# A Mamba2 block with a small MLP: the MLP taken out of the mixer's loop into a phase of its own, the next block's front moved in between the scan's groups

## The chip, the cores and the metric

One Trainium2 chip, one of its cores, float32 in and out. The metric is the device time in microseconds (us) of one launch.

## What is computed

The reference, cut to what matters. `x` is (8, 1024, 256); the `c` modulation gives six rows of 256 for each of the 8 sequences (shift, scale and gate for each of the two halves).

```
xn  = LN(LN(x)*(1+scale_a)+shift_a)                 # LN: mean and variance over the 256
zxbcdt = xn @ in_proj_w                             # 256 -> 1312: z, x, B, C, dt
dt  = softplus(dt + dt_bias); xBC = silu(causal_conv1d(xBC, 4 taps))
y   = ssd_scan(x_ssm, dt, B, C, A)                  # 32 heads of 16, state 128
y   = (y + D*x_ssm) * silu(z);  y = y * rsqrt(mean(y^2)+eps) * rms_w
out = y @ out_proj_w + residual
h   = LN(out); h = relu(h @ mlp_w1 + b1) @ mlp_w2 + b2      # 256 -> 1024 -> 256, the small MLP
x1  = x + gate_a * (h + out)
# feed-forward: ternary weights, 256 -> 2x1024 (silu*gate) -> 1024 gelu -> 1024 gelu -> 256
```

## The kernel before, in words

The work is cut into 16 blocks of 512 tokens (`HALF`): 8 sequences `b`, two halves `u`. A block's 512 tokens lie as four chunks of 128 (`NC`). The program has three stages, each with its own set of engine programs that start together: `mamba` (its short set-up, then its loop), a check of the feed-forward's weights, and the loop of `feed_forward`. Every engine runs its own instructions in order; what passes between engines is counted on semaphores (`Handover`, `Count`). A wait therefore also holds back all that is behind it on the same engine.

**One round of the mixer's loop** (one block), as TensorE sees it:

- ten tiles of the input projection (lines 580 on, six 512-column products each: high and low halves of both operands, `product` at 540). ScalarE empties each tile (743, 745; silu for the z tiles, 750), VectorE runs 15 of the 18 steps of the convolution (981) and GpSimd the other three (833, 836).
- the transposes of dt, the decay and `ec` products (594 on), then the **scan**: four chunks `c` of eight groups `i` (four heads each). For a group TensorE makes the decay matrix (`decay`, 615), ScalarE a relu and an exp of it (779, 785), VectorE the product with `gm` (1089), and TensorE, three groups behind (`LAG`), the contribution `intra` (626). At group 1 of a chunk VectorE reads the last chunk's `yin` (`addends`, 1032, 1041): `yin` exists once, so `intra` of the new chunk waits for that. At groups 3, 4, 6, 7 follow the mean of squares, the residual (1063), the next chunk's operands and the new state.
- the output projection of the last two chunks, with the last residual (1063).
- **the tail, which is the small MLP**: VectorE normalises `o1` (894 to 903), TensorE transposes it (685), eight tiles of `m1` (48 products of 512 columns), ScalarE relu (796), GpSimd rounds to the high half (874), VectorE takes the low half (1121), then `m2` (96 products of 256 columns). Into this tail VectorE also puts the **front of the next block** in five parts: LN of `x` (part 0), scale (1), shift (2), the second LN (3), then `low`, and part 4, the softplus series with the cumulative sum (lines 931 to 950, 20 steps that each wait for the one before). Part 4 ends in `c_cum`, for which ScalarE waits ahead of everything in its next round (736), GpSimd as well (`cleft` copies, 823) and SP too (the `cright` transfers).
- VectorE adds, multiplies by the gate and adds `x` (1133, 1137, 1139), and SP stores `x1_d` (529).

PSUM: four banks `bank` in a ring for everything but the scan's `eb` (two) and `yin`, `yoff`. The front's transposes and dt use the `eb` banks in the tail.

**The weight check** (lines 1194 to 1248) loads the five feed-forward matrices, then ScalarE writes a rounded copy of pieces of 2048 columns (1228), VectorE counts where it differs (1237), TensorE sums. Its result chooses the type of the feed-forward's products. Nothing else runs beside it.

**The feed-forward** (1252 to 1492) is not touched, but for where its weights live and where its semaphores are started.

## Time and profile before

| what | us |
|---|---|
| median of the runs (3) | 3752.67 |
| lowest and highest | 3750.81, 3753.17 |
| span of the profiled execution | 3750.4 |
| TensorE busy in the span | 3007.2 (80%) |
| VectorE busy | 2087.3 (56%) |
| ScalarE, GpSimd busy | 1405.1 (37%), 1073.2 (29%) |

The profiled execution has no device time of its own in the records, so its span stands for it; the median is 2.3 us above the span. The page of the profile cuts the span into 40 equal slices; up to the 24th TensorE is busy for 6 to 8 tenths, from the 26th for 9 or more:

```
PE   1777777687687687686687784699999999999999
DVE  0576 ... (5 to 7 tenths, then 3 to 5)
```

(The second line is shortened in words.) Busy shares are means over a slice; which engine is late in it is seen only in a timeline or in what ended each wait.

### The profile page before, as it was taken

To read this page: it belongs to the slowest core of one execution; us is meant where nothing else is said; L and a number is where in the kernel's file an instruction comes from. 1 tells how busy PE (TensorE), PEld (TensorE's weight loads), DVE (VectorE), ACT (ScalarE), POOL (GpSimd) and SP (SyncE) were. 2 spreads that over 40 slices of the span, in tenths; PEclk is the share of its full clock that TensorE was granted. 3 is DMA by queue.
4 is the path that set the end of the run, shared out by engine and by line. 5 is a ranking of instruction groups with operands and counts; after the bars stand their busy time and mean duration, and the time that the engine had idled before them with its cause. 6 is when DMAs were issued, how large, how long until landed. Compare 5 with 4: busy or idle time off the path is not lost. (4 is left out here: it accounts for less than half of the span.)

```text
span 3750.4 us, 50178 instructions
## 1 busy us (share of the span) xinstructions
PE 3007.2 (80%) x16750; PEld 2270.0 (61%) x16750; DVE 2087.3 (56%) x3938; ACT 1405.1 (37%) x2342; POOL 1073.2 (29%) x1276
## 2 busy tenths in 40 slices
PE   1777777687687687686687784699999999999999
PEld 0455455455355455455455453587887878787877
DVE  5676676677677667667677675433333333333333
ACT  0543553553553553553453452322222222222222
POOL 4333234234234234233233232122222222222222
PEclk6888888888887888888888887799999999999999
DMA  2000000000000001001001002100000000000000
GB/s 92 2 16 6 26 16 15 17 16 24 8 16 30 2 16 30 1 16 30 1 16 30 1 16 96 48 12 13 11 18 18 11 13 11 13 11 13 11 13 17
DMA packets 69811, 72.27 MB, mean 19 GB/s; under 512 B 25816, under 2 KB 64472, under 8 KB 68960
## 3 DMA queue, kind: packets, MB, share of 16 engines
q1 hardware_dynamic: 64480, 69.45, 5.8%
q8 instruction: 110, 1.80, 0.2%
q10 hardware_dynamic: 5120, 0.19, 0.1%
q14 instruction: 101, 0.83, 0.1%
HBM read 51.22 MB, written 28.36 MB: 21 GB/s over the span
## 5 line engine op out<-in xcount | busy, mean ns | idle before, releaser
L1309 PE MATMUL fbank<-hid,fw 128*128 128x512 f32 x4096 | 966.0, 397 | 0.0
L1309 PEld LDWEIGHTS fbank<-hid,fw 128*128 128x128 f32 x4096 | 770.2, 188 | 186.7
L1459 DVE TENSOR_TENSOR hid<-fhf,hid 128x512 fp32r<-128x512 f32 x384 | 264.6, 689 | 708.4 <-POOL hid L1416 708.4
L1416 POOL TENSOR_SCALAR hid<-fhf 128x512 fp32r<-128x512 f32 x384 | 270.3, 704 | 1045.7 <-ACT fhf L1388 765.2
L626 PE MATMUL yin<-mh,xpad 128*32 128x128 f32 x4096 | 353.0, 295 | 188.5 <-DVE mh L1089 110.3
L1388 ACT ACTIVATE fhf<-fbank,sh 128x512 f32<-128x512 f32 x256 | 176.4, 689 | 706.4 <-PE fbank L1309 706.2
L626 PEld LDWEIGHTS yin<-mh,xpad 128*32 128x32 f32 x4096 | 201.9, 115 | 375.9 <-issue 207.6
L1089 DVE TENSOR_TENSOR mh<-hf,gm 128x512 f32<-128x512 f32 x256 | 181.7, 710 | 171.7 <-ACT hf L785 171.7
L850 POOL TENSOR_TENSOR yg<-yin_s,yoff_s 128x512 f32<-128x512 f32 x56 | 84.2, 1503 | 674.5 <-DVE yoff_s L1041 674.5
L1089 DVE TENSOR_TENSOR mh<-cacc,gm 128x512 f32<-128x512 f32 x256 | 175.3, 699 | 145.4 <-ACT cacc L785 137.2
L540 PE MATMUL bank<-ah,wm 128*128 128x512 f32 x512 | 189.0, 449 | 65.2 <-DVE al L956 65.2
L779 ACT ACTIVATE cacc<-eb 128x512 f32<-128x512 f32 x256 | 150.5, 594 | 239.1 <-PE eb L615 239.0
L540 PE MATMUL bank<-wm,hh 128*128 128x256 f32 x1024 | 215.1, 310 | 30.7 <-DVE hl L1121 29.1
L540 PE MATMUL bank<-ah,win 128*128 128x512 f32 x640 | 212.4, 410 | 15.0 <-issue 12.5
L615 PE MATMUL eb<-cright,cleft 99*128 99x512 bf16 x512 | 216.9, 434 | 6.7 <-ACT cacc L779 5.5
L1332 PE MATMUL fbank<-fah,fw 128*128 128x512 f32 x512 | 205.6, 402 | 12.3 <-DVE fhf L1467 8.8
L1332 PE MATMUL fbank<-fal,fw 128*128 128x512 f32 x512 | 203.9, 398 | 0.0
L540 PEld LDWEIGHTS bank<-wm,hh 128*128 128x128 f32 x1024 | 170.5, 206 | 53.4 <-DVE hl L1121 48.4
L540 PE MATMUL bank<-wout,yh 128*128 128x256 f32 x512 | 129.4, 351 | 72.7 <-DVE yl L1046 72.7
L1379 ACT ACTIVATE sa<-fbank,s 128x512 f32<-128x512 f32 x128 | 88.1, 690 | 261.5 <-PE fbank L1332 225.3
L981 DVE SCALAR_TENSOR_TENSOR mh<-cin,cw,mh 128x512 f32<-128x512 f32 x192 | 181.3, 944 | 8.2
L779 ACT ACTIVATE hf<-eb 128x512 f32<-128x512 f32 x256 | 152.3, 595 | 82.5 <-PE eb L615 82.5
(191 smaller groups left out, 5357.5 us busy)
## 6 DMA issues: line engine op xcount, KB each, us to landing
xs<-in_x SPq DMA_DIRECT2D x17, 512.0 KB, 3.5
fx<-x_d SPq DMA_DIRECT2D x17, 512.0 KB, 3.9
h_d<-in_h SPq DMA_DIRECT2D x16, 512.0 KB, 4.9
x_d<-xs SPq DMA_DIRECT2D x16, 512.0 KB, 3.0
fw<-h_d SPq DMA_DIRECT2D x2, 4096.0 KB, 20.7
out_x<-fx SPq DMA_DIRECT2D x16, 512.0 KB, 3.1
w_d<-in_w SPq DMA_DIRECT2D x24, 128.0 KB, 3.9
cright<-parts SPq DMA_DIRECT2D x192, 8.0 KB, 1.9
```

What stands on the lines that cost most here:

```text
L540: mm = pe.matmul(o, left[a], right[c], start=(first and n == 0), stop=(last and n == 2))
L615: mm = pe.matmul(eb[h_eb.slot(key)][:], cleft[:, c, :], cright[c % 2][:, G4 * i:G4 * (i + 1), :].rearrange("k h t -> k (h t)"), start=True ...
L626: mm = pe.matmul(yin[row:row + 2 * HD, h // HQ, :], xpad[c % 2][:, h // 2, h % 2, :, :].rearrange("s w d -> s (w d)"), mh[i % RING][:, j, ...
L779: nc.scalar.activation(es[i % RING].rearrange("s h t -> s (h t)"), eb[h_eb.slot(key)][:], ACT.Relu, scale=-1.0).then_inc(h_eb.free(key), 1)
L981: ins = dve.scalar_tensor_tensor(out=cacc[m][:], in0=cin[:, m, t:t + HALF], scalar=cw[:, m, t:t + 1], in1=cacc[m][:], op0=ALU.mult, op1=AL ...
L1089: dve.tensor_tensor(mh[i % RING][:], es[i % RING], gm[c % 2][:].unsqueeze(1).to_broadcast([P, G4, P]), ALU.mult).then_inc(h_mh.full(key), 1)
L1309: mm = pe.matmul(bank[banks.slot(key)][:], w[:, k, m * P:(m + 1) * P].bitcast(dt), h[:, k, :].bitcast(dt), start=(k + n == 0), stop=(k == ...
L1332: mm = pe.matmul(bank[banks.slot(key)][:], w[:, k, m * P:(m + 1) * P].bitcast(dt), h[:, k, :].bitcast(dt), start=(k + n == 0), stop=(k == ...
L1379: nc.scalar.activation(sa[m % 2][:], bank[banks.slot(key)][:], ACT.Silu, scale=s1[:, m:m + 1])\
L1388: nc.scalar.activation(hf[j % 3][:], bank[banks.slot(key)][:], ACT.Gelu, scale=s[:, m:m + 1]).then_inc(banks.free(key), 1)
L1416: pool.tensor_scalar(hid[i % 2][0][:, m, :], hf[j % 3][:], 1.0, 0.0, ALU.mult, ALU.add)\
L1459: dve.tensor_tensor(hid[i % 2][1][:, m, :], hf[j % 3][:], hid[i % 2][0][:, m, :].bitcast(F32), ALU.subtract).then_inc(c_lo.sem, 1)
```

## The change

It does six things.

1. The MLP leaves the loop. The mixer now ends a block by storing `o1` to DRAM (`o1_d`); `xs` and the gate are no longer needed in the loop, `res` and `parts` get two buffers. `hh`, `hl` and the tail's instructions are gone.
2. The front of the next block sits between groups of the scan: VectorE's parts 0 to 3 behind groups (1,3), (1,6), (2,2), (2,6), `low` behind (3,6); TensorE's two sets of transposes and the dt product behind `intra` of (2,7), (3,1) and (3,3), into a bank `front_bank` of their own; ScalarE's affines at (3,3) and (3,4), its softplus start at (3,7). Part 4 stands after the last residual.
3. The ring of PSUM banks is three instead of four.
4. A new phase `mlp` between mixer and feed-forward runs the 16 blocks unrolled, with two buffers each for `o1` (`ob`) and `x` (`xb`), three tiles for `m1`, one bank for the transposes, four sums for `m2`.
5. ScalarE makes high half and full value itself, by two reads of PSUM; GpSimd instead makes the residual base `(o1 + b2)*gate + x` in three operations of 1024 columns.
6. The weight check is spread over blocks 3 to 13 of the phase, 44 pieces of 512 columns, four a block, at tiles 2 to 5. The stage of its own is gone.

The mixer's part of the diff, cut:

```diff
+FRONT_AT = {"nT0": (2, 7), "affine0": (3, 3), "nT1": (3, 1), "affine1": (3, 4), "low": (3, 6),
+            "dt": (3, 3), "softplus": (3, 7)}
+FRONT_DVE = {(1, 3): 0, (1, 6): 1, (2, 2): 2, (2, 6): 3}
...
-    banks = Handover(sem, "bank", list(mamba_bank_order()), 4)
...
+    banks = Handover(sem, "bank", list(mamba_bank_order()), 3)
+    fronts = Handover(sem, "frontbank", [(u, part) for u in us for part in FRONT_TILES], 1)
...
+                            if (c, i) == FRONT_AT["nT0"]:
+                                front(*after_block(b, u), 0)
+                            if (c, i) == FRONT_AT["nT1"]:
+                                front(*after_block(b, u), 1)
+                            if (c, i) == FRONT_AT["dt"]:
+                                front_dt(*after_block(b, u))
...
+                        if (c, i) == FRONT_AT["affine0"]:
+                            affine(*after_block(b, u), 0)
+                        if (c, i) == FRONT_AT["affine1"]:
+                            affine(*after_block(b, u), 1)
+                        if (c, i) == FRONT_AT["softplus"]:
+                            front_dt(*after_block(b, u))
...
+                        if c in (0, 1):
+                            power(*after_block(b, u), c + 1)
...
+                        if c == NC - 2:
+                            high(*after_block(b, u))
...
+                            if (c, i) in FRONT_DVE:
+                                front(*after_block(b, u), FRONT_DVE[c, i])
+                            if (c, i) == FRONT_AT["low"]:
+                                low(*after_block(b, u))
...
-                    normalise(nrm, o1, b, u, 3 + NC, lambda ins: after(mark(ins))).then_inc(c_norm.sem, 1)
...
+                    front(*after_block(b, u), 4)
```

The phase `mlp`, cut to its loads and to what each engine does in block `n`:

```diff
+MLP_HF = 3
+PIECE = 512
+EARLY = KF - 2
+PIECES = [(i, o) for i, (k, n) in enumerate(FFN_SHAPES) for o in range(0, k * n, PIECE)]
+PIECES_FROM = 3
+PIECES_PER = 4
...
+def pieces_of(n, m):
+
+    p = (n - PIECES_FROM) * PIECES_PER + m - 2
+    return [p] if 2 <= m < 2 + PIECES_PER and 0 <= p < len(PIECES) else []
...
+            def load(n):
+                b, s = n // NU, n % 2
+                if n >= 2:
+                    sp.wait_ge(h_x.free(n), h_x.used_before(0, n))
+                sp.dma_start(ob[s][:], o1_d[b, rows_of(n), :].rearrange("(c p) d -> p c d", p=P))\
+                    .then_inc(h_o.full(n), 16)
+                sp.dma_start(xb[s][:], g["x"][b, rows_of(n), :].rearrange("(c p) d -> p c d", p=P))\
+                    .then_inc(h_x.full(n), 16)
+                if n % NU == 0:
+                    sp.dma_start(gate[b % 2][:], mod_d[b, 2 * D:3 * D].partition_broadcast(P))\
+                        .then_inc(h_gate.full(b), 16)
...
+            load(0)
+            load(1)
...
+            for n in blocks:
+                if n < len(ws):
+                    sp.dma_start(ws[n][:].rearrange("p k n -> p (k n)").bitcast(F32), g["ffn_d"][n])\
+                        .then_inc(s_w[n], 16)
+                sp.wait_ge(c_x1.sem, c_x1.at(0, n + 1))
+                sp.dma_start(x1_d[n // NU, rows_of(n), :].rearrange("(c p) d -> p c d", p=P), xb[n % 2][:])\
+                    .then_inc(h_x.free(n), 16)
+                if n + 2 < MLP_BLOCKS:
+                    load(n + 2)
...
+        @block.tensor
...
+            for n in blocks:
+                for m in range(KF):
+                    key = (n, m)
...
+                if n + 1 < MLP_BLOCKS:
+                    transposes(n + 1, 0)
+                for ks in (range(EARLY), range(EARLY, KF)):
+                    for c in range(NC):
...
+                        if ks[0] == 0 and c == 1 and n + 1 < MLP_BLOCKS:
+                            transposes(n + 1, 1)
...
+        @block.scalar
...
+                    nc.scalar.activation(hh[:, m, :], tile[tiles.slot(key)][:], ACT.Relu, bias=b1c[:, m:m + 1])\
+                        .then_inc(c_hh.sem, 1)
+                    if j >= MLP_HF:
+                        act.wait_ge(c_hl.sem, c_hl.at(0, j - MLP_HF + 1))
+                    nc.scalar.activation(hf[j % MLP_HF][:], tile[tiles.slot(key)][:], ACT.Relu, bias=b1c[:, m:m + 1])\
+                        .then_inc(tiles.free(key), 1)
+                    for p in pieces_of(n, m):
+                        i, o = PIECES[p]
+                        act.wait_ge(s_w[i], 16)
+                        if p:
+                            act.wait_ge(s_count, p)
...
+        @block.gpsimd
...
+                if n + 1 < MLP_BLOCKS:
+                    power(n + 1)
...
+                pool.tensor_tensor(ob[s][:], ob[s][:], b2r[:].unsqueeze(1).to_broadcast([P, NC, D]), ALU.add)\
...
+                pool.tensor_tensor(ob[s][:], ob[s][:], g_, ALU.mult).then_inc(c_base.sem, 1)
...
+                pool.tensor_tensor(ob[s][:], ob[s][:], xb[s][:], ALU.add).then_inc(c_base.sem, 1)
...
+        @block.vector
...
+                    dve.tensor_tensor(hl[:, m, :], hf[j % MLP_HF][:], hh[:, m, :].bitcast(F32), ALU.subtract)\
...
+                    for p in pieces_of(n, m):
+                        dve.wait_ge(s_round, p + 1)
+                        if p:
+                            dve.wait_ge(s_count, p)
+                        dve.scalar_tensor_tensor(out=differs[:], in0=weight(*PIECES[p]), scalar=0.0,
+                                                 in1=rounded[:].bitcast(F32), op0=ALU.add,
+                                                 op1=ALU.not_equal, accum_out=count[:, p:p + 1]).then_inc(s_count, 1)
+                    if n + 1 < MLP_BLOCKS:
                         if m == 1:
...
+                            variances(n + 1)
+                        if m == 5:
+                            normalise(n + 1)
...
+                for c in range(NC):
...
+                    dve.tensor_tensor(xb[s][:, c, :], acc[c][:, 0:D], gate[b % 2][:], ALU.mult)\
...
+                dve.tensor_tensor(xb[s][:], xb[s][:], ob[s][:], ALU.add).then_inc(c_x1.sem, 1)
```

`variances(n + 1)` begins with a wait for the load of `ob` of block n + 1; `transposes` waits for `normalise`.

## Rows read from the trace of the kernel before

**Rows 1.** Windows by stage: stretch, length, busy by engine, PE clock, DMA, GB/s.
```profile
86.60:2322.50 2235.90, 1649.14 (x10436) 1163.48 (x10432) 1551.30 (x3045) 1051.14 (x1875) 730.02 (x833) 0.84 0.05 15
2322.50:2379.30 56.80, 2.17 (x11) 1.67 (x11) 30.30 (x39) 23.62 (x14) 2.07 (x2) 0.50 0.62 228
2379.30:3750.40 1371.10, 1344.91 (x6272) 1101.33 (x6272) 463.22 (x792) 325.77 (x447) 302.69 (x416) 1.00 0.04 13
```

**Rows 2.** Lines 1063 and 1139: ns min/median/max, first and last start.
```profile
L1063 DVE SCALAR_TENSOR_TENSOR o<-bank,rms,res x64: 470/480/485, 156.2 to 2275.3; 128x256 f32<-128x256 f32 x64
L1139 DVE TENSOR_TENSOR xs<-xs,o x16: 1224/1224/1227, 230.2 to 2318.8; 128x1024 f32<-128x1024 f32 x16
```

**Rows 3.** Timeline, end of a scan to the next convolution's end: start, length.
```profile
1298.69 0.48 DVE L1063 SCALAR_TENSOR_TENSOR o<-bank,rms,res 128x256 f32<-128x256 f32 x1 [0.66 <-POOL rms L805]
...
1342.33 0.39 PE L540 MATMUL bank<-ah,win 128*128 128x512 f32 x1
...
1346.62 3.55 DVE L981 SCALAR_TENSOR_TENSOR cacc<-cin,cw,cacc 128x512 f32<-128x512 f32 x3 [0.25 <-ACT cin L745]
1350.20 11.96 DVE L981 SCALAR_TENSOR_TENSOR mh<-cin,cw,mh 128x512 f32<-128x512 f32 x12
1362.23 0.07 DVE L995 MEMSET cin<- 128x18 f32 x1
```

**Rows 4.** Timeline, VectorE's softplus chain, first and last step, then GpSimd.
```profile
1333.58 0.23 DVE L931 TENSOR_SCALAR dden<-dabs 128x128 f32<-128x128 f32 x1 [1.44 <-ACT dabs L730]
...
1340.31 0.23 DVE L950 CAST parts<-crest 128x128 bf16<-128x128 f32 x1
1340.70 5.82 POOL L823 COPY cleft<-parts 32x128 bf16<-32x128 bf16 x12 [9.70 <-DVE parts L950]
```

**Rows 5.** Timeline at a chunk's start; brackets: idle before, releaser.
```profile
1260.52 1.12 DVE L1032 SCALAR_TENSOR_TENSOR yin_s<-xc,dsk,yin 128x128 f32<-128x128 f32 x4
...
1263.44 0.38 PE L615 MATMUL eb<-cright,cleft 99*128 99x512 bf16 x1
...
1264.43 0.62 ACT L785 ACTIVATE hf<-hf 128x512 f32<-128x512 f32 x1
1265.09 0.77 DVE L1089 TENSOR_TENSOR mh<-hf,gm 128x512 f32<-128x512 f32 x1 [2.25 <-ACT hf L785]
```

**Rows 6.** Timeline, GpSimd and VectorE at once, in scan and MLP.
```profile
1279.41 1.27 POOL L852 TENSOR_TENSOR yg<-yg,sz 128x512 f32<-128x512 f32 x1
1280.35 0.89 DVE L1089 TENSOR_TENSOR mh<-hf,gm 128x512 f32<-128x512 f32 x1 [2.14 <-ACT hf L785]
...
1282.98 0.74 DVE L1089 TENSOR_TENSOR mh<-cacc,gm 128x512 f32<-128x512 f32 x1 [1.68 <-ACT cacc L785]
...
1321.93 3.40 POOL L881 TENSOR_TENSOR o<-o,b2r 128x256 f32<-128x256 f32 x4
```

**Rows 7.** Timeline, VectorE, the front's first part in the MLP's stretch.
```profile
1303.92 1.39 DVE L894 BATCH_NORM_STATS2 stats<-xs 128x6 f32<-128x256 f32 x4
...
1307.17 1.96 DVE L903 TENSOR_SCALAR res<-xs,mv,rstd 128x256 f32<-128x256 f32 x4 [1.13 <-POOL rstd L805]
```

**Rows 8.** Groups of instructions: busy us, mean ns of one | idle before.
```profile
L1309 PE MATMUL fbank<-hid,fw 128*128 128x512 f32 x4096 | 966.0, 397 | 0.0
...
L1348 PE MATMUL fbank<-fw,hid 128*128 128x256 f32 x1024 | 129.5, 283 | 11.6 <-DVE hid L1459 11.6
```

**Rows 9.** DMA issues: KB of each, us from issue to landing.
```profile
fx<-x_d SPq DMA_DIRECT2D x17, 512.0 KB, 3.9
...
x_d<-xs SPq DMA_DIRECT2D x16, 512.0 KB, 3.0
```

**Rows 10.** Line 1237, the weight check's comparison: ns min/median/max.
```profile
L1237 DVE SCALAR_TENSOR_TENSOR differs<-fw,rounded x11: 2291/2292/2293, 2330.4 to 2361.9; 128x2048 f32<-128x2048 f32 x11
```

**Rows 11.** Timeline, feed-forward, first load and first product.
```profile
2365.20 0.37 SPq L1270 DMA_DIRECT2D fx<-x_d  x1
...
2379.29 0.79 PE L1332 MATMUL fbank<-fah,fw 128*128 128x512 f32 x1 [3.54 <-DVE fal L1445]
```

573 lines of the change are left out of this document (308 added, 265 removed).

## The prediction

> **What bounds the kernel now.** I first read the windows by stage [rows 1]. The mixer's loop takes 2235.9 us with TensorE busy for 1649.1, the weight check and the feed-forward's start 56.8 us with TensorE idle, the feed-forward 1371.1 us with TensorE busy for 1344.9. The last is bound by TensorE and untouched, so the change is decided in the other two. The mixer's period is read from two source lines [rows 2]: the last additions of the 16 blocks lie from 230.2 to 2318.8, so 2088.6/15 = 139.2 us a block. A timeline then cuts a period in two [rows 3]: the last residual of a scan ends at 1299.2, the next projection begins at 1342.3, the next convolution ends at 1362.2. These 63.0 us hold the MLP; the other 76 us are the rest of the round. All sums below are made against the span of 3750.4 us; the runs' median, 3752.67, is 2.3 above it.
>
> **The mixer's round.** The change replaces the 63.0 us. After the last residual (call it R) VectorE runs part 4, which lay beside m2 before and now lies open: 1333.58 to 1340.54, 7.0 us [rows 4]. Behind its end wait ScalarE (it then empties the projection's tiles, so TensorE stops after three, all the banks there are), GpSimd and SP. ScalarE needs 0.5 us for its two exps and about 1.2 a tile for two tiles, so the convolution starts at R+10. It took 1346.62 to 1362.16, 15.5 us, in a round where all of GpSimd's six conv operations fell beside it [rows 3], as they will again: GpSimd's 5.8 us of copies [rows 4] start at R+7. I add 0.5 for those copies: the convolution ends at R+26. Saved: 63.0 - 26.0 = 37.0 us, in 15 rounds (the last round has no successor): -555.
>
> **What the front costs in the scan.** VectorE's idle time in a chunk is small: 2.25 us before group 3 and 1.68 before group 4 [rows 5, 6], and the first is a latency: `addends` free `yin` at 1261.6, only then comes TensorE's next decay (1263.4), ScalarE's relu and exp, then VectorE (1265.1) [rows 5]. Work put there is hidden; work put elsewhere pushes the whole chain. Statistics take 3.25 us from start to first use, 2.1 of them on VectorE, the normalisation 1.4 to 2.0 [rows 7], an operation of 1024 columns 1.22 [rows 2]. So:
> - part 0 (2.1 us) behind (1,3), against 1.7 idle: +0.5;
> - part 1 (1.4+1.2 and its waits) behind (1,6), nothing idle: +3.0;
> - part 2 (1.2+2.1) behind (2,2), 1.3 more behind GpSimd's gating (1.27) [rows 6], against 3.9 idle: +1.0;
> - the ring of three: the transposes for chunk 3 take the bank of the output projection of chunk 0, freed only by its residual, and the start of the scan waits half a microsecond more for `ec`: +0.8 together;
> - part 3 behind (2,6): +1.4; `low` behind (3,6): +1.3;
> - two affines on ScalarE at (3,3), (3,4), where its exp is the late one; the first hides in its idle time, the second does not: +0.8. The dt product and ScalarE's softplus start find both engines waiting: 0.
> The parts give 8.8; 0.5 is added for `bt` and the waits between dependent steps: +9.3 a round. Bounds: 0 (all hidden) and 16.5 (all of VectorE's 11, ScalarE's 2.6, TensorE's 2.9). 16 x 9.3 = +149. The period becomes 139.2-37.0+9.3 = 111.5.
>
> The last residual of the loop is now at 2275.8 [rows 2]; it moves to 2275.8-555+149 = 1870. Part 4 follows (7.0), then the switch of stages and the semaphores' start, about 2.4 (an estimate; bounds 0.4, a DMA issue, and 4): first load of the MLP at 1879. From such a load to the first product the feed-forward needs 2379.3-2365.2 = 14.1 us [rows 11]; here the two transposes share a bank, +0.5. First m1 product: 1893.6.
>
> **The MLP phase.** TensorE's work in a block: 48 products of 512 columns at 966.0/4096 = 0.236 and 96 of 256 at 129.5/1024 = 0.126 [rows 8], 11.3 + 12.1, and some 1.1 of transposes: 24.5 us. But the order of the waits makes a loop. The load of block n+1 goes into the buffers of block n-1, so it waits for the store of `x1` of n-1. Time zero is TensorE's last product of block n-1:
> - two additions on VectorE and the issue: 2.0; the store lands 3.0 later, the load 3.9 later [rows 9]: `ob` is there at 9.0. VectorE has stood at `variances(n+1)` since m = 1, with hl(2) to hl(7) behind it;
> - variances to 11.2 and `power` to 12.2, as in [rows 7]; hl(2), hl(3) to 12.5;
> - now GpSimd starts its three operations of 1024 columns, twice the 512 that took 1.27: 2.5 us each. Where both engines want SBUF they take turns for whole instructions: GpSimd's gating ran 1279.41 to 1280.68, VectorE's product that started at 1280.35 ended 0.56 after it, 0.89 in place of 0.69 [rows 6]. So hl(4), hl(5) and the normalisation each stand behind one such operation: 12.5 + 3 x 2.5 + 2 x 0.6 + 1.4 = 22.6;
> - only then TensorE's transposes, which stand ahead of m2 in its queue; m1 was done at 11.3. It has idled 11 us. In the check's stage, where it idled too, the granted clock was 0.50, in the dense feed-forward 1.00 [rows 1], so it restarts at the lower level: 1.0 for the transposes, 12.1 + 0.6 for m2 and 1.9 for a slow first part of it (an estimate; bounds 0 and 6, half of m2's time again). Period: 38.2 us.
> In blocks with pieces of the check (11 of 16) ScalarE's rounding for m = 3 waits for the count of m = 2, which is behind `variances`, and so hold tile 4 and 5: hl(4) comes only with that. A piece of 512 columns is a quarter of 2.29 [rows 10] plus fixed time, 0.75 on VectorE and 0.6 on ScalarE, four in series with hl between: +3.4, period 41.6. Block 0 finds its load done and GpSimd's contention all the same (34), block 15 has no successor (24.5). Three blocks at 38.2, eleven at 41.6: 114.6 + 457.6 + 58.5 = 631. The check thus costs 37 here and gives 42 back (2323.6 to 2365.2 was its stage).
>
> **Sum.** 1893.6 + 631 = 2524.6; last addition, store and barrier +5.3, the feed-forward's semaphores now ahead of its load +2.1: 2532; first product +14.1, then 1371.1: 3917 span, 3919 as a run. Over a median of 3752.67 that is +4.4%. Of the old period, 37.0-9.3 = 27.7 is saved in the mixer and about 39 spent in the MLP.
>
> **Rivals.**
> (A, forecast) As above, 3919.
> (B, milder turns) Contention costs as in the MLP of before, where GpSimd's four operations of 256 columns took 3.40 together [rows 6] and VectorE's low halves some 1.1 each: normalisation ends at 17.7, with pieces at 23: periods 33.3 and 38.6. MLP 580, time 3868. For it: those rows; against: no operation of 1024 columns runs on GpSimd there beside two-input work. The Trainium skill, SBUF — State Buffer, "Who interferes with whom", states that whoever issues first holds the shared ports for the whole instruction and the other fully blocks; by that it is A's 3919, by a mere slowing B's 3868.
> (C, the other side: faster) TensorE is the bound of the new phase. If the chain store, load, variances, normalise fits under m1 and the early part of m2, the period is 24.5, the MLP 392 and the time 3680. It decides at a mean period of 40.9 - 167/14 = 29.0 in the 14 middle blocks, below which the change is a gain. For it: two buffers, and every engine's own work is under 24 us; against: load, variances and `power` end at 12.2, four low halves and the normalisation take 3.8 more with nothing contended: 16.0, well after m1's 11.3, and a period of 29.7 without one piece of the check. The Trainium skill's first page, Trainium Kernel Development and Optimization, "Best Practices", says that double buffering overlaps DMA with compute; by that rule it would be C.
> (D, the scan hides the front) Growth 0 to 3 us: 3770 to 3820, slower still by the MLP alone. Against: VectorE's 4 us of idle per chunk, one chunk of them a latency.
> (E, the scan grows to its bound, 16.5): 4034.
>
> **Chances and range.** A 0.48, B 0.22, C 0.13, D 0.09, E 0.08. A part of C with a period near 29 is the only way to no change. Faster by over 0.2% (what a measurement of this kernel tells from no change): 0.12; within: 0.03; slower: 0.85. The range leaves out C and half of E and takes in B with a mixer 4 us a round better than priced, and A with 4 us worse: 3790 to 3990.
>
> **What would show it.** In the changed profile: 16 MLP blocks of 37 to 42 us where TensorE idles 8 to 14 us ahead of the first transposes, released by the normalisation, and TensorE's clock below full in that stage; VectorE idle ahead of `bn_stats` with the load as its releaser; mixer rounds of 109 to 115 us, of which the scan 66 to 72; ScalarE waiting for `parts` at each round's start; the feed-forward's 1371 us unchanged. Wrong it would be if TensorE is busy for 9 tenths in the MLP stage (C), if `variances` does not wait for the load, or if the scan stays at 60.5 us (D).

## The result, and the profile after

The changed kernel takes **3893.7 us** (median of 4 runs, 3889.3 to 3899.9) against 3751.7 before it on the same chip: ratio 1.0379, interval 1.0365 to 1.0394, slower. Forecast were 3919 in a range of 3790 to 3990.

First the page of the profile after: its span and the busy time of each engine.

```profile
span 3891.0 us, 50355 instructions
PE 3032.7 (78%) x16750; PEld 2280.3 (59%) x16750; DVE 2129.8 (55%) x4020; ACT 1496.4 (38%) x2535; POOL 1008.8 (26%) x1100
```

Then the windows by stage, which answer to [rows 1]. They run from the first projection to the last, from there to the MLP's first product, then the MLP with the weight check, then the feed-forward. The columns are those of [rows 1].

```profile
88.40:1793.30 1704.90, 1178.99 (x7500) 757.81 (x7497) 1206.71 (x2428) 877.29 (x1608) 485.85 (x554) 0.81 0.06 18
1793.30:1930.90 137.60, 80.78 (x513) 52.75 (x514) 92.09 (x199) 59.78 (x109) 35.20 (x39) 0.75 0.12 31
1930.90:2526.90 596.00, 423.31 (x2437) 372.16 (x2435) 325.51 (x539) 229.71 (x365) 148.75 (x65) 0.85 0.18 62
2526.90:3891.00 1364.10, 1338.16 (x6272) 1094.22 (x6272) 463.16 (x792) 325.07 (x447) 300.89 (x416) 1.00 0.04 13
```

Before, the loop and the check took 2235.9 + 56.8 = 2292.7 us. Now they take 1704.9 + 137.6 + 596.0 = 2438.5: 145.8 more. The feed-forward is 7.0 shorter. With a start that is 1.8 later, the difference of the spans is 140.6.

**The round.** Its period is 1704.9/15 = 113.7 us, where 111.5 were forecast. Line 1028 is the residual, line 944 the convolution. This is VectorE's timeline over one round's end; it answers to [rows 3].

```profile
1225.81 0.48 DVE L1028 SCALAR_TENSOR_TENSOR o<-bank,rms,res 128x256 f32<-128x256 f32 x1 [0.67 <-POOL rms L778]
...
1233.06 0.23 DVE L912 CAST parts<-crest 128x128 bf16<-128x128 f32 x1
1233.32 0.20 ACT L708 ACTIVATE cend<-cum 128x1 f32<-128x1 f32 x1 [12.00 <-DVE parts L912]
...
1238.61 4.57 DVE L944 SCALAR_TENSOR_TENSOR cacc<-cin,cw,cacc 128x512 f32<-128x512 f32 x3
1243.21 10.81 DVE L944 SCALAR_TENSOR_TENSOR mh<-cin,cw,mh 128x512 f32<-128x512 f32 x12
...
1261.68 0.69 DVE L1054 TENSOR_TENSOR mh<-cacc,gm 128x512 f32<-128x512 f32 x1 [1.12 <-ACT cacc L757]
```

Part 4 lies open for 7.0 us behind the last residual, as forecast, and ScalarE has waited 12 us for `parts`. Three moments cut every round in three: the start of the scan's first product with `gm` (`mh`, line 1054), the start of the last residual and the end of the convolution. The means over 13 rounds (3 to 15), with the kernels of the experiments, are:

| us a round | first `mh` to last residual | last residual to convolution's end | convolution's end to first `mh` | sum |
|---|---|---|---|---|
| before | 68.4 | 63.6 | 7.1 | 139.0 |
| after | 79.0 | 27.0 | 7.6 | 113.6 |
| front_late | 69.2 | 44.2 | 7.6 | 121.1 |
| place | 79.3 | 27.0 | 7.6 | 113.9 |
| dup_stats | 80.2 | 26.9 | 7.6 | 114.7 |
| split4 | 80.2 | 19.6 | 7.6 | 107.4 |
| best | 80.1 | 19.7 | 7.6 | 107.4 |

The five kernels of the next section leave the mixer as it is in after, and their scans take 79.4 to 79.5: a difference of half a microsecond to the 79.0 of after is no effect of an edit. In these five the MLP's first product comes 5 to 8 us later than the 1930.9 of after, too, so a few microseconds between whole runs can't be put down to an edit either.

**The MLP.** Block 1's first product starts at 1966.51, block 2's at 2001.57. VectorE, GpSimd and TensorE in that block:

```profile
1975.53 1.41 DVE L1305 BATCH_NORM_STATS2 mstats<-mo 128x6 f32<-128x256 f32 x4 [4.04 <-DMA mo<-o_d]
1977.58 4.64 DVE L1337 TENSOR_TENSOR mhl<-mhf,mhh 128x512 fp32r<-128x512 f32 x4
1982.14 5.49 DVE L1318 TENSOR_SCALAR mnrm<-mo,mmv,mrstd 128x256 f32<-128x256 f32 x4
...
1977.75 1.39 POOL L1281 TENSOR_TENSOR mrstd<-mvar,neg_half 128x4 f32<-128x4 f32 x1 [27.06 <-DVE mvar L1313]
1979.12 2.55 POOL L1291 TENSOR_TENSOR mo<-mo,b2r 128x1024 f32<-128x1024 f32 x1
1981.75 2.67 POOL L1295 TENSOR_TENSOR mo<-mo,mgate 128x1024 f32<-128x1024 f32 x1
1984.50 2.34 POOL L1298 TENSOR_TENSOR mo<-mo,mx 128x1024 f32<-128x1024 f32 x1
...
1987.68 1.12 PE L1205 MATMUL mfront<-ident,mnrm 128*128 128x128 f32 x4 [9.82 <-DVE mnrm L1318]
```

Times of DVE are VectorE's, of POOL GpSimd's. The chain is the one forecast: load, statistics, root, GpSimd's three operations with VectorE's taking turns, transposes. TensorE waits 9.82 us ahead of them (8 to 14 forecast). In the eleven blocks with pieces of the check the wait is split: 4.0 us stand inside the first product, behind ScalarE's relu, and 6.6 to 6.8 ahead of the transposes, which is under the forecast. In block 5, for one, GpSimd's three operations meet one low half (2.84 us instead of 0.69) and two of the check's comparisons (2.61 and 2.82 instead of 0.68); no normalisation is stopped in any of these eleven. One normalisation of 256 columns takes 407 ns in the median and 2494 where it meets GpSimd. This is line 1318's own view (shortest, median and longest, in ns):

```profile
L1318 DVE TENSOR_SCALAR mnrm<-mo,mmv,mrstd x64: 399/407/2494, 1926.0 to 2469.0; 128x256 f32<-128x256 f32 x64
```

The Trainium skill, SBUF — State Buffer, "Who interferes with whom", says of the ports that VectorE and GpSimd share that whoever issues first has them for the whole instruction and the other fully blocks. The 2494 ns agree: they are what was left of one of GpSimd's operations of 2.3 to 2.7 us, and the normalisation itself.

TensorE's windows of the wait and then of 2 us each at the start of the second product (columns as in [rows 1]):

```profile
1977.50:1988.40 10.90, 1.08 (x6) 0.72 (x5) 10.90 (x11) 3.00 (x5) 8.93 (x4) 0.66 0.22 93
1988.40:1990.40 2.00, 2.00 (x11) 2.00 (x11) 0.51 (x2) 1.45 (x2) 0.00 (x0) 0.50 0.00 0
1990.40:1992.40 2.00, 2.00 (x16) 2.00 (x16) 0.61 (x1) 0.00 (x0) 0.00 (x0) 0.79 0.00 0
1992.40:1994.40 2.00, 2.00 (x21) 2.00 (x19) 0.00 (x0) 0.00 (x0) 0.00 (x0) 1.00 0.03 8
```

After the idle 10 us the product starts at the lower of the two levels (1.2 GHz) and is back at 2.4 GHz in the third window. Periods are 34.4 to 35.6 us in blocks without pieces of the check (34.6 in the mean of blocks 1, 2 and 14) and 37.4 to 37.7 with them (37.5); forecast were 38.2 and 41.6.

### The profile page after: what moved, and what is told of

It reads as the page before. It is cut to its first block and busy times, and to the rows that moved or that the text cites. A ratio compares the mean times of both kernels' runs of the same rounds, so it can differ in the third digit from the quotient of the medians.

```text
span 3891.0 us, 50355 instructions
## 1 busy us (share of the span) xinstructions
PE 3032.7 (78%) x16750; PEld 2280.3 (59%) x16750; DVE 2129.8 (55%) x4020; ACT 1496.4 (38%) x2535; POOL 1008.8 (26%) x1100
## 5 line engine op out<-in xcount | busy, mean ns | idle before, releaser
L623 PE MATMUL yin<-mh,xpad 128*32 128x128 f32 x4096 | 378.9, 312 | 217.6 <-DVE mh L1054 168.9
L623 PEld LDWEIGHTS yin<-mh,xpad 128*32 128x32 f32 x4096 | 214.6, 121 | 410.4 <-DVE mh L1054 217.3
L1054 DVE TENSOR_TENSOR mh<-hf,gm 128x512 f32<-128x512 f32 x256 | 209.1, 817 | 151.2 <-ACT hf L757 149.1
L539 PE MATMUL bank<-ah,win 128*128 128x512 f32 x640 | 232.4, 438 | 71.8 <-ACT cin L717 60.5
L1552 ACT ACTIVATE fhf<-fbank,sh2c 128x512 f32<-128x512 f32 x128 | 88.0, 687 | 382.5 <-PE fbank L1473 382.5
L1496 PE MATMUL fbank<-fah,fw 128*128 128x512 f32 x512 | 204.4, 399 | 11.3 <-DVE fhf L1631 7.8
L1210 PE MATMUL mtile<-mah,wm 128*128 128x512 f32 x512 | 178.8, 422 | 44.0 <-ACT mhf L1264 43.0
L1552 ACT ACTIVATE fhf<-fbank,sh1c 128x512 f32<-128x512 f32 x128 | 88.0, 688 | 320.8 <-PE fbank L1473 320.6
L1210 PE MATMUL macc<-wm,mhh 128*128 128x256 f32 x1024 | 204.0, 301 | 0.0
L539 PEld LDWEIGHTS bank<-ah,win 128*128 128x128 f32 x640 | 135.8, 212 | 112.8 <-ACT cin L717 67.5
L539 PE MATMUL bank<-wout,yh 128*128 128x256 f32 x512 | 143.0, 379 | 75.3 <-DVE yl L1009 69.0
```

The source lines that it names most:

```text
L539: mm = pe.matmul(o, left[a], right[c], start=(first and n == 0), stop=(last and n == 2))
L623: mm = pe.matmul(yin[row:row + 2 * HD, h // HQ, :], xpad[c % 2][:, h // 2, h % 2, :, :].rearrange("s w d -> s (w d)"), mh[i % RING][:, j, ...
L1054: dve.tensor_tensor(mh[i % RING][:], es[i % RING], gm[c % 2][:].unsqueeze(1).to_broadcast([P, G4, P]), ALU.mult).then_inc(h_mh.full(key), 1)
L1210: mm = pe.matmul(o, left[i], right[j], start=(first and t == 0), stop=(last and t == 2))
L1496: mm = pe.matmul(bank[banks.slot(key)][:], w[:, k, m * P:(m + 1) * P].bitcast(dt), h[:, k, :].bitcast(dt), start=(k + n == 0), stop=(k == ...
L1552: nc.scalar.activation(hf[j % 3][:], bank[banks.slot(key)][:], ACT.Gelu, scale=s[:, m:m + 1]).then_inc(banks.free(key), 1)
```

## Experiments on the MLP phase

Theory: the chain above sets the period, not TensorE's work of 24.5 us. Rival: turns between engines and the order of loads cost nothing that TensorE would not take anyway. All comparisons below are with 3893.7, each run having had the kernel before on the same chip at 3751.6 to 3754.6.

**early_load**

```diff
             def load(n):
-                if n >= 2:
-                    sp.wait_ge(h_x.free(n), h_x.used_before(0, n))
                 sp.dma_start(ob[s][:], o1_d[b, rows_of(n), :]...)
+                if n >= 2:
+                    sp.wait_ge(h_x.free(n), h_x.used_before(0, n))
```

> The only edit: the load of block n+2's ob is issued ahead of the wait for block n's x1 store, instead of behind it; the load of xb still waits. In the kernel after, statistics of block n+1 begin 8.5 us into the block and wait on that load in 15 of 16 blocks (56.5 us in all). Turns theory (the chain of addition, store, load, statistics, power, GpSimd's three operations, normalisation, transposes sets the period, which is 35.1 without pieces and 37.6 with): the load lands about 2.8 us earlier, and the whole chain shifts with it, 14 periods by 2.8 = -39 us, total about 3854. TensorE-bound theory (its 24.5 us of work a block is the bound, the rest shadows it): no change, 3894. Port theory (the load would then run beside the eviction and lose what it gains): under -10 us, above 3884.

Measured: 3883.5 us, ratio 1.0344 (1.0327 to 1.0361): -10, a quarter of the 39. VectorE's wait for the load over all blocks fell from 56.5 to 34.9 us, 1.4 a block and not 2.8: the load now took 4.6 us instead of 3.8. It runs beside the store; that this is the reason is not shown. The transposes came 1.5 us earlier in the block, but the period fell by 0.8 (blocks 1, 2 and 14, without pieces) and 1.1 (with). The windows say why: the same ones as above, in the same block.

```profile
1983.62:1993.20 9.58, 1.12 (x6) 0.77 (x5) 9.58 (x9) 2.43 (x5) 7.81 (x4) 0.69 0.16 69
1993.20:1995.20 2.00, 2.00 (x11) 2.00 (x10) 0.51 (x2) 1.45 (x2) 0.00 (x0) 0.50 0.00 0
1995.20:1997.20 2.00, 2.00 (x12) 2.00 (x11) 0.56 (x1) 0.00 (x0) 0.00 (x0) 0.50 0.00 0
1997.20:1999.20 2.00, 2.00 (x17) 2.00 (x17) 0.00 (x0) 0.00 (x0) 0.00 (x0) 0.91 0.00 0
```

The product began earlier and stayed at the lower clock for one window more; it took 13.8 us instead of 13.1 here, 13.8 instead of 13.3 in the mean of blocks 1 to 14. A part of what the load gained was so paid back by TensorE.

**base_first**

```diff
-                if n + 1 < MLP_BLOCKS:
-                    power(n + 1)
                 pool.wait_ge(h_o.full(n), h_o.filled(0, n))
...
                 pool.tensor_tensor(ob[s][:], ob[s][:], xb[s][:], ALU.add)
+                if n + 1 < MLP_BLOCKS:
+                    power(n + 1)
```

> The only edit: GpSimd's three 1024-column operations of block n (about 7.7 us, 2.6 each) are placed ahead of its power for block n+1 in program order, so that they run while the load of ob is still under way instead of beside VectorE's hl copies and normalisation. Turns theory: hl(4), hl(5) (each about 2.3 late) and the first normalisation (2.49 instead of 0.40) are then not behind GpSimd; about 6 us a block of the chain go, 14 blocks: -85 us, total about 3808; the longest normalisation falls well under the 2.49 us that it took. If GpSimd is then itself late with power (its three operations end after the statistics), less: -3 a block, 3850. Theory that turns between the two engines cost nothing: 3894, within 10 us.

Measured: **3804.1 us**, ratio 1.0132 (1.0115 to 1.0149): -90, where 85 were expected. Periods are 26.8 us in block 1, 29.4 and 29.5 in blocks 2 and 14, and 31.4 on average with pieces. The timeline of block 1 (it starts at 1967.23):

```profile
1977.84 2.50 DVE L1337 TENSOR_TENSOR mhl<-mhf,mhh 128x512 fp32r<-128x512 f32 x4
...
1980.26 1.38 DVE L1318 TENSOR_SCALAR mnrm<-mo,mmv,mrstd 128x256 f32<-128x256 f32 x4
...
1981.69 0.66 PE L1205 MATMUL mfront<-ident,mnrm 128*128 128x128 f32 x4 [3.11 <-DVE mnrm L1318]
1981.78 3.32 POOL L1289 TENSOR_TENSOR mo<-mo,b2r 128x1024 f32<-128x1024 f32 x1 [2.38 <-DVE mnrm L1318]
...
1983.87 1.78 DVE L1324 TENSOR_TENSOR mal<-maf,mah 128x512 fp32r<-128x512 f32 x1 [1.03 <-ACT mah L1251]
```

The four low halves fell from 4.64 to 2.50, the normalisation from 5.49 to 1.38. The expectation placed GpSimd's three operations under the wait for the load; in fact the first starts right behind the normalisation (1981.78) and all three lie beside TensorE's second product. Turns are still taken there (line 1324, 1.78 us), but nothing waits for them. The wait is now 3.1 us, and the median of a transpose fell from 421 to 273 ns.

**pieces_out**

```diff
-    p = (n - PIECES_FROM) * PIECES_PER + m - 2
-    return [p] if 2 <= m < 2 + PIECES_PER and 0 <= p < len(PIECES) else []
+    if m not in (0, 1, 6, 7):
+        return []
+    p = (n - PIECES_FROM) * PIECES_PER + (0, 1, 6, 7).index(m)
+    return [p] if 0 <= p < len(PIECES) else []
```

> The only edit: the four pieces of the weight check of each block stand at groups m = 0, 1, 6, 7 of the first product instead of 2, 3, 4, 5. Blocks with pieces have a period 2.7 us longer than those without (37.6 against 34.4 to 35.6), though VectorE and TensorE have idle time in each. If that is the pieces' place (ahead of evictions and hl copies that the next transposes wait for): 11 blocks by up to 2.7 = -30 us, total about 3864. If it is their amount of VectorE work, wherever it stands: 3894, within 8 us.

Measured: 3868.8 us, ratio 1.031 (1.0293 to 1.0327): -25. Blocks with pieces now take 34.8 on average, blocks 1, 2 and 14 without them 34.6. The 2.9 us more that they took in after was the pieces' place in VectorE's order, not their amount of work.

**mlp_all**: the three edits together.

> The three edits of early_load, base_first and pieces_out together; nothing else. If the chain sets the period until TensorE's own 24.5 to 26 us a block does: periods fall from 35.1/37.6 to 25 to 28, about 14 by 10.5 = -150 us, total about 3740 (3715 to 3775), the clock in this stage rises above the 0.86 that it had. If the three gains overlap (the same wait removed thrice), no more than the best of the three alone: about 3810.

Measured: **3729.4 us**, ratio 0.9941 (0.9925 to 0.9958): -164, and below the kernel before. The MLP's stage in its windows, and VectorE's groups of lines for the load's wait:

```profile
1936.10:2362.10 426.00, 384.31 (x2434) 342.03 (x2434) 315.67 (x539) 225.11 (x363) 154.65 (x63) 0.96 0.26 86
```
```profile
L1307 DVE BATCH_NORM_STATS2 mstats<-mo 128x6 f32<-128x256 f32 x64 | 22.5, 414 | 23.9 <-DMA mo<-o_d 23.9
```

TensorE is busy for 384.3 of 426.0 us at a granted clock of 0.96; the periods are 24.8 to 25.7 but for two (28.5, 27.1). Here rival C of the prediction holds: TensorE is the bound but for some 1.5 us a block, in which it still waits for the normalisation. The second product takes 11.9 us, as it would at the full clock.

The three alone sum to -124, together they gave -164. The traces show the phase by itself: from the MLP's first product to its last it takes 574.9 us in after, 561.2 in early_load, 482.4 in base_first, 544.7 in pieces_out and 404.9 in mlp_all. That is 136 us for the three alone and 170 together, so 34 of the 40 lie in the phase; the other 6 are no more than what whole runs differ by. One more run tells where they come from.

**base_pieces**: mlp_all without early_load.

> The edits of base_first and pieces_out together, without early_load: mlp_all less early_load. Alone, early_load gave only 10 us of the 39 forecast, while its three edits together gave 164, 40 more than the sum of the three. Give-back theory: alone, its shorter wait for the transposes was partly paid back by TensorE, which still began the second product at the lower clock and stayed there longer; with base_first the wait is short and the product begins at the full clock, so the earlier load is worth its full 2 to 3 us a block: this kernel has periods of about 28 in all blocks, 3 over those of mlp_all, and takes 3729 + 39 = 3768 (3760 to 3775). Rival: early_load is worth 10 anywhere and the 40 come from base_first and pieces_out together: 3740.

Measured: 3769.1 us, ratio 1.0035 (1.0024 to 1.0047), the time that the give-back theory gave. Periods are 28.4 on average with pieces. So the earlier load was worth 40 us here and 10 alone (41.7 and 13.7 in the phase); base_first and pieces_out sum to -114 alone and gave -125 together. Again the windows of a second product, that of block 5, behind a wait of only some 4 us:

```profile
2088.80:2093.78 4.98, 0.78 (x6) 0.41 (x5) 4.80 (x15) 3.52 (x6) 1.71 (x2) 1.00 0.00 0
2093.78:2095.78 2.00, 2.00 (x15) 2.00 (x14) 2.00 (x4) 1.16 (x2) 2.00 (x1) 0.66 0.00 0
2095.78:2097.78 2.00, 2.00 (x11) 2.00 (x11) 2.00 (x2) 0.80 (x2) 1.92 (x2) 0.50 0.00 0
2097.78:2099.78 2.00, 2.00 (x19) 2.00 (x19) 2.00 (x1) 0.00 (x0) 1.92 (x2) 0.98 0.00 0
```

and of the same block's second product in mlp_all:

```profile
2078.49:2090.37 11.88, 11.88 (x103) 11.88 (x102) 11.02 (x11) 3.42 (x5) 8.44 (x3) 1.00 0.00 1
```

The clock still falls behind that wait, only later, inside the product of this block. Over blocks 1 to 14 the product takes 13.3 us in base_pieces (12.0 to 14.4) and 12.1 in mlp_all, where the wait is 1.5 us in the mean and only one block of 14 shows it. So the earlier load moves the start of the second product by 1.5 us a block alone and by 1.9 here, and the product's length takes 0.5 from the former and adds 1.1 to the latter: 1.0 against 3.0 a block, 14 and 42 us over 14 blocks. The give-back theory had the time right and its reason in part: it wanted base_pieces' second product to begin at the full clock and stay there, and of 14 blocks three did so, in four the granted clock was full through the transposes and then fell, and in seven it had fallen ahead of them. The wait's length alone doesn't decide that: with waits of 3.1 to 3.3 us the product took 12.0 us in blocks 1, 10 and 14 and 14.3 in block 11. What decides it is shown by no run here.

## Experiments on the mixer

Theory: work of VectorE in the scan costs about itself wherever it stands, and the tail is set by part 4. Rivals: the places of parts 1 and 3; the ring of three banks. The expectations put the scan's growth at 11.95 us; the means of 13 rounds give 10.6, and 11.1 with the stretch between the convolution's end and the first `mh`.

**front_late** puts the front back behind the scan (TensorE's, ScalarE's and GpSimd's shares of it likewise); the MLP keeps its phase.

```diff
-                            if (c, i) in FRONT_DVE:
-                                front(*after_block(b, u), FRONT_DVE[c, i])
-                            if (c, i) == FRONT_AT["low"]:
-                                low(*after_block(b, u))
...
                     residual(NC - 1)
+                    for part in range(4):
+                        front(*after_block(b, u), part)
+                    low(*after_block(b, u))
                     front(*after_block(b, u), 4)
```

> Undoes one part of the change: the MLP stays in its own phase, but the whole of the next block's front (VectorE parts 0 to 3 and low, GpSimd's roots and high copies, TensorE's transposes and dt product, ScalarE's affine and softplus) stands behind the scan, as it did before. The ring stays at three banks and the front keeps its bank. Front-work theory: the scan, which grew by 11.95 us, falls back by 10 to 12, and the tail grows by the chain of statistics 2, root 1.5, normalise and scale 2.6, shift and statistics 3.2, root 1.5, normalise 1.4, transposes 1, affine and low 3, dt and softplus 3, about 19 us open: +7 a round, 15 rounds, about +105, total about 4000 (3960 to 4050). Ring theory: what the scan lost is the fourth bank's; then it falls back by under 4, the round is +15, total about 4120. If the front behind the scan hides beside the last chunk's products: about 3900, and spreading it was worth nothing.

Measured: **4010.8 us**, ratio 1.068 (1.0662 to 1.0698): +117 against after. From the table: the scan falls by 9.8 to 69.2, within 0.9 us of before, and the tail grows by 17.2. So the ring of three (with whatever else differs from before in a scan without front work) costs 0.9 a round there and 0.5 ahead of the first `mh` (7.6 against 7.1), and the front's work costs 9.8. VectorE's timeline of the tail, from the last residual to the convolution (line 937):

```profile
1281.87 0.48 DVE L1021 SCALAR_TENSOR_TENSOR o<-bank,rms,res 128x256 f32<-128x256 f32 x1 [0.67 <-POOL rms L772]
1282.27 1.40 DVE L844 BATCH_NORM_STATS2 stats<-xs 128x6 f32<-128x256 f32 x4
...
1294.37 1.11 PE L549 MATMUL front_bank<-ident,nrm 128*128 128x128 f32 x4 [13.37 <-DVE nrm L856]
...
1300.39 0.23 DVE L886 TENSOR_SCALAR dden<-dabs 128x128 f32<-128x128 f32 x1 [0.50 <-ACT dabs L697]
...
1311.25 2.64 DVE L937 SCALAR_TENSOR_TENSOR cacc<-cin,cw,cacc 128x512 f32<-128x512 f32 x3 [0.42 <-ACT cin L714]
```

The front takes 18.1 us in the open (1282.3 to 1300.4), 19 expected. This run also splits the change in two. Moving the MLP out, with all else that the change does but for spreading the front, takes the kernel from 3754.4 to 4010.8; spreading the front over the scan gives 117 of that back. In the loop the MLP cost 17.9 us a round (139.0 against 121.1), in its own phase some 36 a block.

**place**

```diff
-FRONT_DVE = {(1, 3): 0, (1, 6): 1, (2, 2): 2, (2, 6): 3}
+FRONT_DVE = {(1, 2): 0, (1, 3): 1, (2, 2): 2, (2, 3): 3}
```

> The only edit: the next block's front parts 0, 1, 2, 3 are emitted on VectorE after scan groups (1,2), (1,3), (2,2), (2,3) instead of (1,3), (1,6), (2,2), (2,6). The scan part of a round grew by 11.95 us with the change. If it grew because parts 1 and 3 stand where VectorE has no slack before a chunk's end (growth 5.1 at group (2,4), 8.85 at (2,7)): -3.5 a round, 16 rounds, -56 us, total about 3837. If every microsecond of VectorE work put into the scan costs about itself wherever it stands: 3894, within 10 us.

Measured: 3896.1 us, ratio 1.0388 (1.0371 to 1.0406): no change. The scan is 79.3 against 79.0. The four places together are not cheaper; the table below takes them apart.

**dup_stats** (the added instructions write a buffer that nobody reads, so nothing computed changes)

```diff
                 if part == 0:
                     dve.wait_ge(xin.full(u), xin.filled(b, u))
+                    for c in range(NC):
+                        dve.bn_stats(stats2[:, c, :], xs[:, c, :])
```

> The only edit: front part 0, in the scan after group (1,3), makes its four statistics instructions twice, the added ones into a buffer of their own that nobody reads: 1.4 us more VectorE work a round. If VectorE's program order is what sets the scan from there on (so that front work costs about itself wherever it is put, as the run with the other places suggests): +1.4 a round, 16 rounds, +22, total about 3916. If TensorE or ScalarE sets it and VectorE has slack there: 3894, within 6 us.

Measured: 3909.5 us, ratio 1.0405 (1.0388 to 1.0423): +16, of which some 3 are the other chip's (before took 3754.4 there, 3751.7 beside after), and the interval overlaps that of after. The trace is clearer: the scan is 1.2 a round longer than after's and 0.7 longer than in the five kernels with after's mixer, for 1.4 of added work, so the added work costs half of its length or more. It is nearer to the first theory (+22) than to the second (0).

Where in the scan the growth arises can be read from the starts of VectorE's products with `gm`: how much later than in the kernel before each comes, counted from the scan's first, in the means of the same 13 rounds. Part 0 stands behind (1,3) in after, part 1 behind (1,6), part 2 behind (2,2), part 3 behind (2,6), the affines at (3,3) and (3,4), `low` behind (3,6).

| us later than before, at group | (1,4) | (1,7) | (2,1) | (2,2) | (2,6) | (2,7) | (3,3) | (3,4) | (3,7) |
|---|---|---|---|---|---|---|---|---|---|
| after | 0.2 | 3.3 | 3.4 | 5.0 | 7.5 | 8.8 | 8.7 | 9.4 | 10.6 |
| early_load (mixer as after) | 0.6 | 3.7 | 3.7 | 5.5 | 8.0 | 9.3 | 9.2 | 9.9 | 11.1 |
| place | 2.2 | 2.2 | 2.3 | 3.7 | 9.0 | 9.1 | 8.9 | 9.6 | 10.8 |
| dup_stats | 1.3 | 4.4 | 4.4 | 6.1 | 8.7 | 10.0 | 9.9 | 10.6 | 11.8 |
| front_late | 0.2 | 0.2 | 0.2 | 0.5 | 0.9 | 0.9 | 0.8 | 0.8 | 0.8 |

In dup_stats the added work shows at (1,4), right behind its place, and stays: part 0 had used up what was idle there. Place isn't neutral in its parts. Its parts 0 and 1 cost 2.3 up to (2,1) instead of 3.4, and its parts 2 and 3 cost 6.8 up to (2,7) instead of 5.4. No run has the first two where place has them and the last two where after has them, so whether that would be cheaper is untested.

**rms_first**

```diff
-                        if c in (0, 1):
-                            power(*after_block(b, u), c + 1)
                         if c:
                             rms_power(b, u, c - 1)
+                        if c in (0, 1):
+                            power(*after_block(b, u), c + 1)
```

> The only edit: in GpSimd's loop over chunks, the root of the previous chunk's mean square goes ahead of the next front's power instead of behind it, in chunks 0 and 1. In the kernel after, residual 0 of a round comes late, and with a ring of three banks for the scan's products the next one, bank<-ident,xc, waits 4.16 us for it. If GpSimd's power (1.41 us there) in front of the root is what makes it late: -0.7 to -1.4 a round, -11 to -22 us, total 3872 to 3883. If it is VectorE's front part 0: 3894, within 6 us.

Measured: 3885.5 us (-8), ratio 1.0357 (1.0339 to 1.0374). The interval overlaps that of after, so this isn't told apart from nothing; the scan's 78.7 a round is 0.3 under that of after. TensorE's waits for the bank that residual 0 frees went down by 10 us in 16 rounds, here in the groups of lines, first of after, then of rms_first:

```profile
L604 PE MATMUL bank<-ident,xc 128*128 128x128 f32 x64 | 21.7, 340 | 60.3 <-DVE o L1028 60.3
```
```profile
L604 PE MATMUL bank<-ident,xc 128*128 128x128 f32 x64 | 21.7, 340 | 50.1 <-DVE o L1028 50.1
```

The wait of 3.8 us a round on the ring is real, but front_late, which has 32.7 us of it, scans about as fast as before: so most of it seems to be time that TensorE has.

**split4**: part 4's first seven steps go ahead of the last residual but one, the rest ahead of the last square mean. (GpSimd waits for its own last root before it goes on.)

```diff
                     square_mean(NC - 2)
+                    front(*after_block(b, u), 4)
                     residual(NC - 2)
                     y_halves(NC - 1)
+                    front(*after_block(b, u), 5)
                     square_mean(NC - 1)
                     residual(NC - 1)
-                    front(*after_block(b, u), 4)
```

> The only edit: part 4 of the next front (softplus polynomial, cumulative sums, decay parts, 14.6 us on VectorE) is cut in two, and the first seven steps stand ahead of the next to last residual, the rest (with the cumulative sums) ahead of the last square mean, instead of all behind the last residual; GpSimd waits for its own last root before it goes on. Theory A: the open softplus chain of 7.0 us ahead of the convolution, with the wait for the banks behind it, starts the next round; moved ahead of the last residual it is covered by waits for TensorE and GpSimd there: the convolution starts 4 to 6 us earlier relative to the last output of the scan, -64 to -96 us, total 3798 to 3830. Theory B: the last residual is late by just what part 4 takes and the convolution's products were not waiting for part 4: 3894, within 15 us. Theory C: VectorE's chain at the scan's end is full, the split adds its waits: +1 to +3 a round, 3910 to 3940.

Measured: **3794.0 us**, ratio 1.0128 (1.0105 to 1.0151): -100, a little beyond the best of theory A. Its timeline of a round's end:

```profile
1274.79 1.26 DVE L904 SCALAR_TENSOR_TENSOR dser<-dser,dsq 128x128 f32<-128x128 f32 x4
...
1278.69 0.23 DVE L917 CAST parts<-crest 128x128 bf16<-128x128 f32 x1
1278.84 0.15 DVE L1024 TENSOR_SCALAR ms<-bank 128x1 f32<-128x1 f32 x1
1278.95 0.20 ACT L708 ACTIVATE cend<-cum 128x1 f32<-128x1 f32 x1 [5.95 <-DVE parts L917]
...
1279.66 0.48 DVE L1033 SCALAR_TENSOR_TENSOR o<-bank,rms,res 128x256 f32<-128x256 f32 x1 [0.67 <-POOL rms L778]
...
1281.93 2.33 DVE L949 SCALAR_TENSOR_TENSOR cacc<-cin,cw,cacc 128x512 f32<-128x512 f32 x3 [1.31 <-ACT cin L717]
```

The steps now lie where VectorE had idled, for TensorE's last output product and for GpSimd's root. The latter wait is in the groups of lines, first of after, then of split4:

```profile
L1028 DVE SCALAR_TENSOR_TENSOR o<-bank,rms,res 128x256 f32<-128x256 f32 x64 | 30.8, 482 | 66.7 <-POOL rms L778 66.7
```
```profile
L1033 DVE SCALAR_TENSOR_TENSOR o<-bank,rms,res 128x256 f32<-128x256 f32 x64 | 30.8, 482 | 24.7 <-POOL rms L778 24.1
```

It fell by 42 us. `parts` is ready 0.7 us ahead of the last residual instead of 7.5 behind it, and the convolution starts 2.3 us behind the residual instead of 12.8. These two rounds flatter the edit, for the rounds alternate: 2.3 and 7.1 us in split4, 10.2 and mostly 12.8 in after, in the mean 4.5 instead of 11.6. The tail falls by 7.4 and the scan grows by 1.2 in the mean.

**both** (mlp_all, place and split4) and **best** (mlp_all, split4 and rms_first):

> The edits of mlp_all, place and split4 together. If they are independent, the sum of what those show alone: by the estimates above about -150 - 56 - 80 = -286, total about 3610 (3580 to 3700), under both kernels. If moving the front's work only trades VectorE time for VectorE time, the mixer stays and the total is that of mlp_all, about 3740.

> The edits of mlp_all, split4 and rms_first together, without those of place. Measured alone against the kernel after, these gave -164, -100 and -8, sum -272: 3622 if they add up. With place in the set (3650) the mixer's period was 109.1 us against 107.95 with split4 alone; if place costs that 1.2 us a round, the total here is 3650 - 19 - 6 = 3625. If place was harmless and the two sets of edits interact otherwise: 3645.

Measured: both 3650.5 us, ratio 0.9728 (0.9712 to 0.9744), and **best 3624.9 us, ratio 0.9659 (0.9643 to 0.9675)**. The single gains of the latter, 164 + 100 + 8 = 272, add up to its 269. Both is 18 us above the sum of its parts, and best, without place, isn't: place, free by itself, costs 1.3 us a round here: the mixer's period, from first projection to first projection, is 109.1 in both and 107.8 in best. Why it does so only beside split4 is not shown. The stages of best, from its windows:

```profile
87.90:1833.00 1745.10, 1256.44 (x8012) 810.24 (x8009) 1292.57 (x2628) 944.48 (x1719) 535.20 (x596) 0.78 0.07 20
1833.00:2256.20 423.20, 382.21 (x2434) 340.15 (x2434) 318.73 (x539) 225.16 (x363) 154.50 (x63) 0.97 0.26 87
2256.20:3621.20 1365.00, 1339.34 (x6272) 1094.79 (x6272) 463.59 (x792) 325.37 (x447) 302.46 (x416) 1.00 0.04 13
```

So the change as made is 3.8% slower, and the same change with these orders altered is 3.4% faster than the kernel before.

## Why the prediction was right, and where its terms were off

The mechanism and the sign were right: the mixer saves less than a phase of its own for the MLP costs, because that phase runs at the pace of a chain. Forecast were 27.7 us saved a round and 39 spent a block; measured are 25.3 (139.2 against 113.9) and 35.9 (574.9/16). In spans the sum was 3917 and the trace has 3891. That it comes so near is in part luck: the mixer was put 37 us too short up to the MLP's first product, the MLP 56 too long, the feed-forward 7 too long.

- **The tail** was priced at R+26 from the last residual's end; measured 26.5 (27.0 from its start). Part 4 open for 7.0, ScalarE waiting, the convolution's 15.4: all as forecast.
- **The scan's growth** was mis-sized: 9.3 forecast, 10.6 + 0.5 measured. The table by groups shows which terms held: part 0 (0.5 forecast, 0.2 measured), part 1 (3.0, 3.1), part 3 (1.4, 1.3), the affines (0.8, 0.7) and `low` (1.3, 1.2). The step that failed is part 2's "against 3.9 idle: +1.0". Between (1,7) and (2,6) the scan grows by 4.2, of which front_late has 0.7 without any front work. VectorE's idle time ahead of (2,3) and (2,4), 2.3 and 1.7 us before, is used up as the prediction wanted, but 3.0 us of new idle time stand ahead of (2,2), (2,5) and (2,6), all released by ScalarE's exp. Work put there hides in one wait and opens others; what holds the exp back is open. The ring was priced at 0.8, the later `ec` included, and front_late has 0.9 + 0.5.
- **The mixer's end.** By the table this and 0.5 in the tail make 2.3 a round. The period from last residual to last residual is 113.9, not 111.5, which makes some 35 us in 15 rounds, and the first round is 5 longer than priced; from the last residual to the MLP's first product it took 21.2, not 23.6. So that product came at 1930.9, not 1893.6.
- **The MLP** from first product to the feed-forward's first product: 652.5 forecast (631 + 7.4 + 14.1), 596.0 measured. In the blocks without pieces the load stood in `ob` at 8.5 (9.0 forecast) and the first product ended at 11.4 (11.3). The transposes came at 20.9, not 22.6. The second product took 13.1, not 12.1 + 0.6 + 1.9 = 14.6: at full clock 11.9, and its slow part 1.2. That GpSimd's three operations each stop VectorE once is right, and so is their price: uncontended, rival C had 16.0 and A 22.6, 6.6 for the turns, and from after to base_first the transposes came 6.4 earlier. What was too long is the uncontended chain, 16.0 against base_first's 14.5. In blocks 1, 2 and 14 they stopped one low half and two of the four normalisation operations, where two low halves and one of these were forecast. The pieces cost 2.9 and not 3.4 a block.
- **The feed-forward** was put at 1371.1 as before and took 1364.1: 7 less. Why is open.
- **Rival B** (milder turns, 3868) is as near to the measured time as A, and its MLP of 580 us is much nearer to the 575 measured than A's 631. That is no credit to its mechanism: the turns are whole instructions (2494 ns), and A was some 3.5 us a block too long in its other terms. The total time alone would not have told the two apart. **Rival C** was wrong for this kernel and right for mlp_all. The Trainium skill, Trainium Kernel Development and Optimization, "Best Practices", says that double buffering overlaps transfers with compute. In after it did so in part only, in mlp_all's order nearly: with the same two buffers TensorE was busy for 423.3 of 596.0 us after, and for 384.3 of 426.0 there, and by early_load the load's own place is the smaller part of that. **D** falls with the scan's 79.0. **E** falls too: the growth is 11.1 and not 16.5.

## What to carry to other kernels

A stage taken out of a loop loses the other stages' work as cover, so its own chain must be read before its engine sums are. Here each of the four delays was an order in a queue: a load behind a store's wait, slow GpSimd operations beside the work that TensorE waits for, check pieces ahead of low halves, a dependent chain behind the last output instead of in its waits. Price a reordering together with the others: an earlier load was worth 10 us alone and 40 with the rest, another placement 0 alone and 18 lost in a tighter round. A total that comes out right doesn't prove its terms: here errors of some 40 and 60 us nearly cancelled, and a rival with the wrong mechanism came as near.

## What the hardware showed that was not expected

- A shorter wait doesn't always give its full length back. Behind 10.9 us with next to no work on TensorE the second product was back at the full clock in its third window of 2 us; behind 9.6 us the third window's mean was still 0.91. Behind 3.0 to 4.2 us it was the same in kind but not in each block: the clock fell in 11 of 14 blocks of base_pieces, ahead of the product or inside it, and the product took 12.0 to 14.4 us. Behind 1.5 us in the mean it fell in one of 14 (mlp_all), and the MLP stage's granted clock was 0.96 there, 0.85 in after.
- Which of GpSimd's operations hold VectorE up depends on the operation. After shows both in its alternating rounds: beside the twelve small copies into `cleft` the convolution's first three operations took 2.41 us (1349.72; 2.33 in split4, 1281.93); beside GpSimd's 128x512 additions and the scaling ahead of them they took 4.57 (1238.61). Beside the copies it was GpSimd that lost: they took 6.21 us in split4 (1279.86) and 3.89 where VectorE was idle for most of them (after, 1233.46). The whole convolution takes about as long in both (15.7 and 15.4 us in 13 of 15 rounds), since GpSimd's additions then meet its later operations.
